# Queries, keys and values from five one-pass float32r products over 128 rows instead of float32 products over two halves of 96, in a vision layer of patch tokens, linear attention and routed experts

## The reference, cut to what matters

```python
h = tokens(x)                                     # (16, 256, 192)
xn = layernorm(h)
q, k, v = split(xn @ w_inp + b_inp)               # 12 heads of 16; the change is in this product
s = einsum(q or k, omega) * 16 ** -0.25           # 16 features a head; diag = sum(s) / 2
qf = exp(s - diag - max over features) + EPS      # keys: max over heads and features
a = cumsum(kf * v) . qf / (cumsum(kf) . qf + EPS) # running sums over a group of positions
h = h + a @ w_out + b_out
h = h + experts(layernorm(h)) + spectral term
```

## Time and profile before

| | us |
|---|---|
| median of 3 runs | 733.06 (731.43 to 738.74) |
| the profiled execution | 734.74 |
| its span, first to last instruction | 733.0 |
| PE busy in the span | 663.8 (91%) |
| DVE busy | 508.2 (69%) |
| POOL busy | 450.1 (61%) |
| ACT busy | 439.7 (60%) |

### The profile page before, as it was taken

The page is one execution under the profiler, slowest core; times in us unless marked ns, Lnnn a source line. Parts: engine busy times, 40 slices in busy tenths (PEclk is TensorE's granted clock), DMA queues, the critical chain, the costliest instruction groups (busy, mean ns, idle before and its releaser), DMA issues. The chain is left out here.

```text
span 733.0 us, 17468 instructions
## 1 busy us (share of the span) xinstructions
PE 663.8 (91%) x4943; PEld 609.1 (83%) x4944; DVE 508.2 (69%) x1508; ACT 439.7 (60%) x867; POOL 450.1 (61%) x478
## 2 busy tenths in 40 slices
PE   3687999999999999999963899999999999998993
PEld 2556588888888888888961699999999999998993
DVE  3124358888888888888844479988889868865651
ACT  1022677766666666667611477777767767765771
POOL 7773334666666666666544447677776757857844
PEclk9789999999999999999975799999999999999998
DMA  8317122323333333332010424333353364463423
GB/s 177 88 20 223 50 72 80 80 80 79 79 79 79 79 79 79 79 79 70 26 53 4 100 30 63 62 56 58 67 66 65 56 127 57 74 127 54 68 37 32
DMA packets 63364, 53.77 MB, mean 73 GB/s; under 512 B 25318, under 2 KB 57722, under 8 KB 63322
## 3 DMA queue, kind: packets, MB, share of 16 engines
q0 software_dynamic: 19168, 23.48, 19.2%
q1 hardware_dynamic: 44154, 29.84, 16.6%
HBM read 29.72 MB, written 21.99 MB: 71 GB/s over the span
## 5 line engine op out<-in xcount | busy, mean ns | idle before, releaser
L1290 POOL DMA_INDIRECT result<-e_y,e_tag x78 | 130.8, 1676 | 83.1 <-DVE e_y L1594 42.2
L1337 PE MATMUL e_yp<-x_w2s,e_hh 128*128 x468 | 140.1, 367 | 3.7 <-DVE e_y L1594 2.0
L1586 DVE TENSOR_TENSOR e_hl<-e_hid,e_hh 128x512 fp32r<-128x512 f32 x117 | 80.4, 689 | 62.4 <-ACT e_hh L1398 61.5
L533 POOL DMA_INDIRECT tbl_dram<-c_entry,a_slot x64 | 64.5, 1008 | 87.8 <-DVE c_entry L1097 62.0
L1390 ACT ACTIVATE e_hid<-e_hidden,e_b 128x256 f32<-128x256 f32 x234 | 102.4, 474 | 26.5 <-PE e_hidden L1324 8.7
L1338 PE MATMUL e_yp<-x_w2s,e_hl 128*128 x468 | 117.9, 252 | 0.0
L1398 ACT CAST e_hh<-e_hid 128x512 fp32r<-128x512 f32 x117 | 72.5, 621 | 64.6 <-PE e_yp L1338 64.6
L629 PEld LDWEIGHTS a_ab<-a_values,a_masked 128*128 128x128 f32 x768 | 94.5, 191 | 13.4 <-issue 11.5
L629 PE MATMUL a_ab<-a_values,a_masked 128*128 (+1 forms) x768 | 100.1, 271 | 3.3 <-DVE a_masked L953 3.1
L1263 POOL DMA_INDIRECT e_x<-x_dram,e_tag x78 | 83.2, 1066 | 28.9 <-issue 22.6
L1337 PEld LDWEIGHTS e_yp<-x_w2s,e_hh 128*128 128x128 f32 x468 | 88.9, 190 | 4.6 <-issue 4.6
(11 more groups left out here) (251 smaller groups left out, 1562.9 us busy)
## 6 DMA issues: line engine op xcount, KB each, us to landing
a_raw<-in_ew SPq DMA_DIRECT2D x16, 288.0 KB, 3.1
h_dram<-x_w2s SPq DMA_DIRECT2D x8, 384.0 KB, 3.4
c_hb<-h_dram SPq DMA_DIRECT2D x16, 192.0 KB
a_raw<-in_ew SPq DMA_DIRECT2D x16, 192.0 KB, 2.6
a_raw<-in_ew SPq DMA_DIRECT2D x32, 96.0 KB, 2.6
result<-c_hb SPq DMA_DIRECT2D x16, 192.0 KB
x_dram<-a_xn SPq DMA_DIRECT2D x16, 192.0 KB
result<-e_room POOLq DMA_DIRECT2D x4, 768.0 KB, 8.8
```

The source lines that it names most:

```text
L1290: pool.indirect_dma_start(out=out, in_=y[:, i % YR, j], in_offset=None, out_offset=bass.IndirectOffsetOnAxis(ap=tag[:, i % TR, j, 0:1].bit ...
L1337: pe.matmul(Y[:, j, 0:2 * D], hh[:, f, c], w(f, 2 * D), start=f == 0, stop=False, skip_group_check=True)
L1586: g.tensor_tensor(hl[:, f:f + 2].rearrange("p f t -> p (f t)"), hid[:, f:f + 2].rearrange("p f t -> p (f t)"), hh[:, f:f + 2].rearrange("p ...
```

## The change

What it does, part by part:

1. The normed tokens `xn` are written 256 columns wide: columns 0 to 191, and behind them columns 128 to 191 again (four `tensor_scalar` in `apply1` where there were two). Their four transposes then fill all 128 rows of `R[0]`.
2. ACT rounds the transposed tokens to float32r (`xh`), in the place of the float32 copy `xn_t`. A new `low_x` on DVE makes `xl`, the rest, in two instructions between `place` and `project`.
3. The weights `wqkv` are float32r in four tiles of 128 rows: high part of rows 0 to 127, low part of the same, the last 64 rows with bias and their low part stacked, and a fourth for `xl`. `products` takes five one-pass matmuls for each block of tokens, for queries and keys (408 columns) and for values (192 columns); the fourth waits for `xl_ready`.
4. In the tokens block the fold has three groups of four products in place of two, interleaved with `t1`; all three are moved out by DVE, which splits them (four instructions each). The loaded weights are wider (`wqk_t` 320 columns for 193, the values 128 x 3 x 192).
5. `rest` is gone: POOL writes the low part of `raw1[:, 1]` in place, SP stores it from there, and waits for that store before it loads the next `raw1`.
6. `sheet` is gone: the table lies in `feat[0]`, so POOL sets it up after its last scatter and not at the start.
7. POOL's setup of the attention block makes the constant rows of `xl`: four more instructions, one fewer.
8. `dynamic_dma_scratch_size` goes from 4096 to 2048.

```diff
-        groups = [("t2", k) for k in range(8)] + [("fold", 0), ("fold", 1)] + [("t1", k) for k in range(4)] + \
-            [("p2", 0), ("p1", 0), ("p1", 1)] + [("mix", k) for k in range(8)]
+        groups = [("t2", k) for k in range(8)] + [("fold", 0), ("t1", 0), ("fold", 1), ("t1", 1), ("fold", 2), ("t1", 2)] + \
+            [("p2", 0), ("t1", 3), ("p1", 0), ("p1", 1)] + [("mix", k) for k in range(8)]
...
+            def split_weights(k, ps):
+
+                high = (0, 2, 3)[k]
+                rows = (slice(0, P), slice(EMB, P), slice(96, 97))[k]
+                low = 1 if k == 0 else high
+                folded = float(DH) ** -0.25
+                dve.tensor_scalar(wqkv[:, high, 0:QK], ps[:, 0:QK], folded, None, ALU.mult).then_inc(split_step, 1)
+                dve.tensor_copy(wqkv[:, high, QK:], raw_v[:, k]).then_inc(split_step, 1)
+                dve.wait_ge(split_step, 3 * k + 2)
+                dve.tensor_tensor(wqkv[rows, low, QK:], raw_v[rows, k], wqkv[rows, high, QK:].bitcast(F32), ALU.subtract
+                                  ).then_inc(split_step, 1)
+                return dve.scalar_tensor_tensor(out=wqkv[rows, low, 0:QK], in0=ps[rows, 0:QK], scalar=folded,
+                                                in1=wqkv[rows, high, 0:QK].bitcast(F32), op0=ALU.mult, op1=ALU.subtract)
...
-        xn = sb("xn", [P, TJ, D])
-        xn_t = sb("xn_t", [KH + 1, 2, T])
+        xn = sb("xn", [P, TJ, XW])
+        xh, xl = sb("xh", [P, 2, T], F32R), sb("xl", [P, 2, T], F32R)
...
-        sheet = sb("sheet", [1, 448])
+        sheet = feat[0][0:1].rearrange("p h f -> p (h f)")
...
                         wait_apart(sp, s["low1"], 2 * i)
                         store_rest(i - 1)
+                        wait_apart(sp, s["rest_out"], 16 * i)
...
-            g.memset(xn_t[KH:KH + 1], 1.0).then_inc(s["setup"], 1)
+            constant = att[:].rearrange("p j d -> p (j d)")[EMB:P, 0:T]
+            g.memset(constant, 0.0).then_inc(s["setup"], 1)
             pool.wait_ge(s["setup"], 3)
+            for row in (0, 32):
+                g.memset(constant[row:row + 1], 1.0).then_inc(s["setup"], 1)
+            pool.wait_ge(s["setup"], 5)
+            g.tensor_copy(xl[EMB:P, 1], constant).then_inc(s["setup"], 1)
+            pool.wait_ge(s["setup"], 6)
...
-            for n in range(3):
-                g.memset(sums[n], 0.0).then_inc(s["table_set"], 1)
-            g.iota(tile_no, [[1, NTILE]], base=0, channel_multiplier=0,
-                   allow_small_or_imprecise_dtypes=True).then_inc(s["table_set"], 1)
...
-                    if not (fixed(i) and i == 0):
-                        pool.wait_ge(s["rest_out"], 16 * i)
                     wait_apart(pool, s["high1"], 2 * i + 2)
                     g.tensor_tensor(unit(w1l), raw1[:, 0], unit(w1h).bitcast(F32), ALU.subtract).then_inc(s["low1"], 1)
-                    g.tensor_tensor(rest[:], raw1[:, 1], unit(w1s).bitcast(F32), ALU.subtract).then_inc(s["low1"], 1)
+                    g.tensor_tensor(raw1[:, 1], raw1[:, 1], unit(w1s).bitcast(F32), ALU.subtract).then_inc(s["low1"], 1)
             sched(pool, emit)
+            pool.wait_ge(s["state_done"], B)
+            for n in range(3):
+                g.memset(sums[n], 0.0).then_inc(s["table_set"], 1)
+            g.iota(tile_no, [[1, NTILE]], base=0, channel_multiplier=0,
+                   allow_small_or_imprecise_dtypes=True).then_inc(s["table_set"], 1)
             pool.wait_ge(s["scattered"], 16 * 4 * B)
...
+                def products(to, j, columns):
+
+                    rows = slice(j * P, (j + 1) * P)
+                    for n, (x, w) in enumerate(((xh[:, 0], 0), (xh[:, 0], 1), (xh[:, 1], 2), (xl[:, 0], 0), (xl[:, 1], 3))):
+                        if n == 3:
+                            pe.wait_ge(s["xl_ready"], 2 * (i + 1))
+                        last = pe.matmul(to, x[:, rows], wqkv[:, w, columns], start=n == 0, stop=n == 4)
+                    return last
+
                 def qk(j):
-                    for c in range(2):
-                        last = pe.matmul(R[1 - j][:, 0:2 * H * HW], xn_t[0:KH + c, c, j * P:(j + 1) * P],
-                                         wqkv[0:KH + c, c, 0:2 * H * HW], start=c == 0, stop=c == 1)
-                    last.then_inc(s["qk_done"], 1)
+                    products(R[1 - j][:, 0:2 * H * HW], j, slice(0, 2 * H * HW)).then_inc(s["qk_done"], 1)
...
-                norm_apply(hb[:, b % 4], mv, rstd1, xn, "norm_step", "xn_ready", "rstd1_ready", b)
+                dve.wait_ge(s["rstd1_ready"], 2 * (b + 1))
+                for j in range(TJ):
+                    for at, columns in ((D, slice(P, D)), (0, slice(0, D))):
+                        h1 = hb[:, b % 4, j, columns]
+                        last = v.tensor_scalar(xn[:, j, at:at + h1.shape[1]], h1, mv[:, j, 0:1], rstd1[:, j:j + 1],
+                                               ALU.subtract, ALU.mult)
+                    last.then_inc(s["xn_ready" if j else "norm_step"], 1)
...
+            def low_x(i):
+                dve.wait_ge(s["xnT_out"], i + 1)
+                v.tensor_tensor(xl[:, 0], R[0][:, 0:T], xh[:, 0].bitcast(F32), ALU.subtract).then_inc(s["xl_ready"], 1)
+                v.tensor_tensor(xl[0:EMB, 1], R[0][0:EMB, T:2 * T], xh[0:EMB, 1].bitcast(F32), ALU.subtract
+                                ).then_inc(s["xl_ready"], 1)
...
                 if choice:
                     place(i - 3)
+                if one:
+                    low_x(i)
                 if tail:
                     project(i - 2)
```

73 lines of the change are left out of this document (40 added, 33 removed).

## The result

The kernel after takes 752.2 us (median of 4 runs, 748.2 to 756.6) against 735.9 us (4 runs) of the kernel before beside it: ratio 1.0225, interval 1.012 to 1.033. I had forecast 739.7 us with a range of 729 to 749. The measured time lies above that range: 16 us more than the kernel before beside it, where I had forecast 6.6 more. The same kernel run later (`after_again`) gave 1.0218. Two of the four executions took 748 us, just inside the range, and two 756, at a mean granted clock of 0.942 instead of 0.950; the profile is of one at 748, and where the other two lose 8 us no trace shows.

The account below looks back on a forecast made before the run. A cycle of DVE's stretch and some PE work was taken to bound the loop. Loop 2.8, first turns -0.8, setup 0.8, tokens 1.5, table 2.3 made +6.6 us: 741.3 us profiled, 739.7 us median, range 729 to 749.

Parts of the forecast that it names:

- The cycle: Attention loop: 14.7 us of DVE and 3.4 us of PE set a turn of about 18.1 to 18.3 us.
- the wider `xn`: Attention loop, `apply1` on DVE: two more `tensor_scalar` at 0.24 us each cost 0.47 us a turn (0.2 to 0.7).
- `low_x` is free: Attention loop: its two DVE instructions, 0.76 to 0.84 us, fit the 1.16 us wait for `project` and cost nothing.
- PE bounds the loop: Rival for the attention loop: all 16 turns would give 1.1 us, -13 us in sum, 720 us; chance 0.12.
- `raw1` in place: Attention loop: `raw1` loads about 1.6 us later, costing nothing; rival that it comes late: 755 us, chance 0.08.
- The table: Before the experts: its 4.6 us on DVE move behind POOL's last scatter, costing +2.3 us (1.8 to 3).
- The products: Attention loop: `qk` five in 0.85 us, values ten in 1.2; PE saves 1.1 us, gain 0.22 us a turn.
- The scratch memory: Halved descriptor memory: nothing taken, with few transfers in flight; rival that it is too small: over 750 us, chance 0.03.
- The tokens block: Folds and weights end PE's first part 3.2 us later, against a 1.66 us wait for gathers: +1.5 us (0 to 3.5).
- First three turns: Start of the attention loop: DVE waits for PE there, so part of PE's saving arrives, -0.8 us (0 to -2).
- Setup: Attention setup on POOL: new constant rows take 1.4 us against 0.6, costing +0.8 us (0.4 to 1.3).
- The clock in the range: Whole kernel: one change of the clock window, about 1.7 us, was included in the range 729 to 749 us.

Follow-up runs that it names:

- experiment 8: POOL's low parts of the first weights wait until `apply1` is written: 757.98 us, 1.0352 on the changed, rearranged kernel at scratch 4096; 731.6 us, 0.9982 on the kernel before.
- before_again: The kernel before, unchanged, run and profiled once more: 733.72 us, ratio 1.0012.
- b_scratch: The kernel before with only the DMA scratch halved from 4096 to 2048: 740.99 us, ratio 1.0143.
- b_wide_xn: The kernel before with only two more `tensor_scalar` of 64 columns a turn in `apply1`, result unread: 738.33 us, ratio 1.0087.

## Why the prediction was wrong, and where it was right

Right, with its sizes:
- **The cycle.** DVE's stretch and 3.4 us of PE set the full turn: +0.47 for the wider `xn` (0.43 and 0.44 measured, taken out and put in), -0.22 for the products (0.21), +0.25 in sum (18.55 - 18.33 = 0.22). `low_x` is free, with 0.35 us left in front of L1084. The rival "PE bounds the loop" is out: PE has 0.9 us less work and the turn grew.
- **`raw1` in place** costs nothing in a full turn, but it is not free of waits: ACT idles 0.85 us for it in the plain turn of after, and not at all in the full turns of before. ACT's work is not in the cycle, so this stays hidden until the load comes later still (experiment 8).

```profile
210.33 0.51 ACT L906 CAST x_w1h<-a_raw 128x384 f32 x1 [0.85 <-DMA a_raw<-in_ew]
```
- **The table**, +2.3, measured 1.9: from the end of POOL's last scatter to the experts it is 3.1 us before (394.97 to 398.12) and 5.0 after, 5.0 to 5.1 in the other profiles with the change and 1.7 to 3.2 in those without. The stage's length did not show it, since from ACT's last copy to the end of the last scatter it took 46.2 us instead of 48.1, in which the lower clock had 18 us instead of 21; in `before_again` it is 46.1, with 15 us.
- **The products** are right in sum only: five of 408 columns take 1.08 us (0.85 forecast), ten of 192 take 1.09 (1.2). PE saves 0.9 us, not 1.1.

Wrong:
- **The scratch memory: "with few transfers in flight I take nothing".** This is the step that failed. Alone, on the kernel before, it costs 1.4% (0.8 to 2.1%), 8.3 us between the medians and 10 by the ratio; taken out of the measured 752.2 us, that would leave 742 to 744, inside the range. In after's profile: 0.85 us for the turn of the 57th and 3.8 for that of the 85th, 4.7 of the loop's 7.4; the other 2.7 are 0.21 us in each of 12 turns and 0.2 in the first three. It is the largest single error in that profile, 4.7 of 6.9. The rival was written down and got 0.03. Its price, "over 750", is near the 752.2 by luck: half the scratch alone gives 741. And of the places it named, the gathers did wait, but of the 156 transfers of the experts one was late and that block got no longer; the scatters of the loop, which it did not name, cost most. No row spoke for it, and none against: what I used, that few transfers are in flight, is no statement on how many have been issued. The Trainium skill knows the scratch as a part of SBUF that is set aside for the descriptors' ring (SBUF — State Buffer, section "SBUF size: 192, 224, or 256?"), at 16 KiB; no run here has that size. At 4096 none of these waits stands in the trace, at 3072 three do, at 2048 five.
- **The tokens block: +1.5** became +4.1. The folds (+1.4 for 1.5) and the weights (+1.7) arrived as forecast. But PE's chain got 4.7 us longer, not 3.2, with a group of products (L258) that waits 0.76 us for ACT's copy of the transposes now in front of it, and a second stretch at the lower clock of 10.2 us instead of 6.8. And the 1.66 us subtracted for the wait at the second half were not all slack against the gathers: from the first half to the second it is 8.76 us in before and 8.20 in every profile with the changed stage, with the gathers on time or late, so only 0.6 could be gained. 4.7 - 0.6 = 4.1. The late gathers are not in this sum; by `b_scratch` they would allow a start at 63.7, and PE comes at 64.50. The lower clock had a quarter of this block in before (mean 0.88), not half as I wrote.
- **First three turns: -0.8** became +0.2: the saving of PE in them did not come through. ACT waits 2.15 and 1.14 us for `raw1` in the second and third turn of after (0.82 us and not at all in before); whether that is what takes the saving back no run separates.
- **Setup: +0.8** was +1.0 for POOL, and 1.3 more for the clock.
- **The clock in the range.** The 1.7 us for one change of the clock come from no row. Between the two profiles of the kernel before the setup differs by 1.4 us (7.54 and 6.11), with 3.4 us at the lower level in one and none in the other.
- **Sum of the errors**: loop 5.4, tokens 2.6, setup 1.5, table and experts -2.6; 6.9 us, which is 13.5 - 6.6. The rest of the 12.5 us by which the median was missed is mostly the step from the profiled execution to the median: I took 1.7 us off, and the median lies 3.6 above.

## What to carry to other kernels

A size in the program's head is an edit like any other. If nothing in the trace prices it, run it alone before all else, and until then give it a chance that reflects ignorance, not hope; the SBUF that it frees can cost more than the code it makes room for. These waits came by the number of indirect DMAs issued, so count what a queue has been given in all.

A wait in front of an instruction is slack only down to the next thing that it would wait for: of the 1.66 us in the token stage 0.6 was. A bound that is taken away shows what stood right behind it: here PE's chain and the gathers in the token stage, DVE and then PE with ACT in the loop, `raw1` behind POOL. Before an engine's saving or an overlap is booked, name the second-latest and its distance.

## What I had not expected

- The late indirect DMAs come by number: the 25th, 41st, 57th, 85th and 260th in all five profiles at 2048, whatever else was changed.
- A wait of 2 us of POOL costs the loop up to 4.5, and TensorE's clock falls where it costs more than itself: in after, behind the 85th ACT idles 1.1 us and PE 0.9 us, and then the lower level comes. At the 57th the clock stays at 1.00 in after, and 1.4 us of wait cost 0.85.
- In the token stage the granted clock can decide more than the change. Five profiles have before's token stage with its gathers on time. Four have a mean of 0.87 to 0.90 up to the attention, and it starts at 68.0 to 68.9 us; the fifth (`b_wide_xn`) has 0.82, and it starts at 74.4 us. With the changed stage and 4096 the same holds: 0.86 and 71.9 or 73.9 us, 0.80 and 78.5.
- The executions in which the kernel before takes 776 us instead of 733 lose most of it in the token stage. `after_again` is 27.4 us longer than after, 21.7 of them in the token stage, 5.9 in the experts and none in the loop; of the kernel before no such profile was kept. PE's matmuls stand apart by up to 2.2 us there, a few by more, with nothing waited for, in all seven profiles of the two groups. In `after_again`:

```profile
49.65 1.44 PE L254 MATMUL tk<-x_w2s,t_w 48*64 48x256 f32 x3 [1.80 <-issue]
...
56.01 1.31 PE L254 MATMUL tk<-x_w2s,t_w 48*64 48x256 f32 x2 [2.21 <-issue]
```
What holds PE up there is open. The ratio of after to before is the same in both kinds, 1.0225 and 1.0218, but a rearrangement of PE's work in that stage is not: 0.9961 and 0.9985 in the one, 1.0136 in the other.
